# Float32 attention queries by five products of 64 columns, in place of a zero fill and fifteen bfloat16 products

## The reference

```python
x = _layernorm(x + _L0_gnn_ref(x, edge_index, ...))    # two sage_conv layers, relu between
Qh = (x @ Wq.T + bq).reshape(n, H, D)                  # H = 4 heads of D = 16
Kh, Vh = (x @ Wk.T + bk).reshape(n, H, D), (x @ Wv.T + bv).reshape(n, H, D)
Ee = (edge_attr @ We.T + be).reshape(-1, H, D)
score = (Kh[src] * Qh[dst] * (1.0 / np.sqrt(D)) * Ee).sum(-1)
score = jnp.exp(jnp.clip(score, -5.0, 5.0))
msg = Vh[src] * score[..., None]
wV = jax.ops.segment_sum(msg, dst, num_segments=n)
out = _layernorm(x + wV.reshape(n, H * D))
```

## Time and profile before

| | us |
|---|---|
| median of 3 runs | 13896.76 (13885.14 to 13908.0) |
| the profiled execution | 13876.17 |
| its span | 13874.4 |

### The profile page before, as it was taken

How to read it: one execution, slowest core, us unless ns; L and a number is a source line. 1 busy time by engine, 2 the same in 40 slices (tenths; PEclk the granted TensorE clock), 3 DMA queues, 4 the chain that set the end, 5 groups by cost and what they waited for, 6 DMA issues and landing times.

```text
span 13874.4 us, 192542 instructions
## 1 busy us (share of the span) xinstructions
PE 7655.9 (55%) x51633; PEld 6718.6 (48%) x51634; DVE 4877.0 (35%) x11774; ACT 2823.4 (20%) x4770; POOL 7767.2 (56%) x8221
## 2 busy tenths in 40 slices
PE   5556656566666555566655555444444544444554
PEld 4555545555555445455544545444444444444444
DVE  3333333333333323233333334333333333433334
ACT  1111111111111000000000003333333333333333
POOL 5555655555555555555555555555555555555554
PEclk7666666766666666666666666555555555555555
DMA  3222222222222112111111112333333333333333
GB/s 62 50 55 52 53 50 50 49 50 49 49 49 49 42 41 46 41 42 43 41 40 41 40 40 82 101 97 98 101 95 98 98 99 90 101 92 93 99 93 82
DMA packets 951617, 917.13 MB, mean 66 GB/s; under 512 B 484896, under 2 KB 740544, under 8 KB 950544
## 3 DMA queue, kind: packets, MB, share of 16 engines
q0 software_dynamic: 260000, 369.16, 12.8%
q1 hardware_dynamic: 605345, 430.43, 11.6%
q10 hardware_dynamic: 85325, 105.63, 2.2%
HBM read 789.35 MB, written 115.24 MB: 65 GB/s over the span
## 4 chain that ended last, share of the span: by engine, by line
PE 30%; issue 30%; another core or an unknown queue 23%; DVE 7%; DVEq 7%; ACT 2%; ACTq 0%; DMA 0%; POOL 0%; POOLq 0%; SPq 0%
PE ps_kv L763 4%; PE ps_kv L754 3%; PE ps_e L740 3%; PE ps_sum L723 2%; PE ps_q L723 2%; PE ps_kv L923 2%; PE ps_hot L723 2%; PE ps_t L732 1%; ACT node_q L1037 1%; PE ps_kv L772 1%; PE ps_sum L923 1%; PE ps_hot L923 1%; PE ps_kv L903 1%; PE ps_q L923 1%
## 5 line engine op out<-in xcount | busy, mean ns | idle before, releaser
L627 POOL DMA_INDIRECT kv<-kv_rows,src_ids x3125 | 2955.6, 946 | 2344.0 <-DVE message L1520 1412.2
L627 POOL DMA_INDIRECT kv<-in_x,src_ids x2500 | 2365.3, 946 | 1845.4 <-issue 912.1
L627 POOL DMA_INDIRECT kv<-h_rows,src_ids x2500 | 2367.1, 947 | 1801.5 <-issue 955.6
L754 PE MATMUL ps_kv<-between,hot 128*128 128x490 bf16 x2500 | 897.8, 505 | 976.2 <-ACT node_q L1037 553.9
L723 PE MATMUL ps_sum<-kv,hot 128*128 128x65 f32 x5000 | 937.9, 355 | 247.7 <-issue 210.5
L723 PEld LDWEIGHTS ps_sum<-kv,hot 128*128 128x128 f32 x5000 | 922.8, 277 | 270.9 <-issue 270.2
L1086 ACT ACTIVATE node_h<-node_h,unit 128x640 bf16<-128x640 f32 x722 | 1042.6, 1444 | 36.9 <-issue 8.1
L723 PE MATMUL ps_hot<-kv 128*128 128x65 f32 x1880 | 418.9, 400 | 1075.4 <-issue 885.8
L723 PEld LDWEIGHTS ps_hot<-kv 128*128 128x128 f32 x1880 | 391.7, 309 | 1148.8 <-issue 1146.7
L754 PEld LDWEIGHTS ps_kv<-between,hot 128*128 128x128 bf16 x2500 | 291.4, 130 | 1305.9 <-issue 995.8
L1306 DVE TENSOR_SCALAR between<-ps_t,message 128x980 bf16<-128x980 f16 x1250 | 898.7, 719 | 0.0
(11 more groups left out here) (253 smaller groups left out, 12432.2 us busy)
## 6 DMA issues: line engine op xcount, KB each, us to landing
node_h<-in_dst SPq DMA_DIRECT2D x625, 320.0 KB
node_q<-in_edge_attr SPq DMA_DIRECT2D x125, 480.0 KB
edge_space<-ee_rows SPq DMA_DIRECT2D x125, 480.0 KB
kv<-kv_rows,src_ids POOLq DMA_INDIRECT x3125
kv<-in_x,src_ids POOLq DMA_INDIRECT x2500
node_q<-in_edge_attr SPq DMA_DIRECT2D x125, 320.0 KB
kv<-h_rows,src_ids POOLq DMA_INDIRECT x2500
edge_space<-ee_rows SPq DMA_DIRECT2D x125, 320.0 KB
```

The lines of the kernel that those rows point to most:

```text
L627: nc.gpsimd.indirect_dma_start(out=into_slot, out_offset=None, in_=table_rows, in_offset=bass.IndirectOffsetOnAxis(ap=ids, axis=0),).then_ ...
L754: mm = nc.tensor.matmul(bank, place_hot[:, k, :], pair_hot[:, k, half * HALF * W:(half + 1) * HALF * W], start=(k == 0), stop=(k == K - 1))
```

## The change

Queries are kept in float32, and TensorE multiplies them with float32 one-hots.

- `queries32` (float32, 64 columns a block) lies over `node_q`; VectorE writes it, without `raw_queries`, without waits for room. `split_queries` and its semaphores go; ScalarE and VectorE wait for `d_kvq.read` in their place.
- `hotT` and `hotT_x` become float32, `q_block` 64 float32 columns. The Square reads `edge_ids` with the stride of five elements and writes `hotT` directly, the Relu works in place there; `apart` and the wait for the previous Relu go.
- `query_rows` issues five products a group in place of fifteen, and as many for an extra block in place of fifteen.
- The zero fill (L910) goes. `sum_messages` starts the bank (start=True) and doesn't end it when queries follow (`last`), so that the first query product of a column writes and later ones add. The three starting products (L951) stay open likewise.

```diff
@@ -118,6 +118,7 @@
 
         tiles_a, tiles_b = ((end - first) * EE_A for first, end in PARTS)
         sums_space = node_q[:].rearrange("p b f -> p (b f)").bitcast(F32)
+        queries32 = sums_space[:, 0:NB * D].rearrange("p (b f) -> p b f", b=NB)
         at = EE_A * 2 * PAIRS * D
         attr = sums_space[:, 0:at].rearrange("p (i f) -> p i f", i=EE_A)
         edge_space = sb("edge_space", [P, max(tiles_b, SLOTS) * K * D], F32)
@@ -181,20 +182,18 @@
         at = SLOTS * K * P
         hot32_x = after_h[:, at:at + K * P].rearrange("p (k n) -> p k n", k=K)
         at += K * P
-        hotT_x = after_h[:, at:at + K * P // 2].bitcast(BF16).rearrange("p (k n) -> p k n", k=K)
-        at += K * P // 2
-        q_block_x = after_h[:, at:at + ROW // 2].bitcast(BF16)
-
-        at += ROW // 2
+        hotT_x = after_h[:, at:at + K * P].rearrange("p (k n) -> p k n", k=K)
+        at += K * P
+        q_block_x = after_h[:, at:at + D]
+        at += D
 
         edge_ids = after_h[:, at:at + SLOTS * K * P].bitcast(I32).rearrange("p (u e) -> p u e", u=SLOTS)
         at += SLOTS * K * P
-        hotT = after_h[:, at:at + SLOTS * K * P // 2].bitcast(BF16).rearrange("p (u k e) -> p u k e", u=SLOTS, k=K)
-        at += SLOTS * K * P // 2
-        q_block = after_h[:, at:at + SLOTS * ROW // 2].bitcast(BF16).rearrange("p (u f) -> p u f", u=SLOTS)
-        at += SLOTS * ROW // 2
-        apart, apart_x = after_h[:, at:at + K * P], after_h[:, at + K * P:at + 2 * K * P]
-        assert at + 2 * K * P <= NB * 2 * D
+        hotT = after_h[:, at:at + SLOTS * K * P].rearrange("p (u k e) -> p u k e", u=SLOTS, k=K)
+        at += SLOTS * K * P
+        q_block = after_h[:, at:at + SLOTS * D].rearrange("p (u f) -> p u f", u=SLOTS)
+        at += SLOTS * D
+        assert at <= NB * 2 * D
         squares = after_h[:, NB * D:].rearrange("p (b f) -> p b f", b=NB)
 
 
@@ -676,28 +670,11 @@
                 z = node_x[:, c * CH:(c + 1) * CH, D:2 * D]
                 nc.gpsimd.tensor_tensor(z, z, over_features(std[:, c * CH:(c + 1) * CH]), ALU.mult).then_inc(d.normed, 1)
 
-            def split_queries(c):
-                raw, rest = raw_queries[:, c % 2], raw_queries[:, 2]
-                into = node_q[:, c * CH:(c + 1) * CH, :]
-                pool.wait_ge(d_kvq.read, c + 1)
-                nc.gpsimd.tensor_copy(into[:, :, 0:D], raw).then_inc(split_step, 1)
-                pool.wait_ge(split_step, 3 * c + 1)
-                nc.gpsimd.tensor_tensor(rest, raw, into[:, :, 0:D], ALU.subtract).then_inc(split_step, 1)
-                pool.wait_ge(split_step, 3 * c + 2)
-                nc.gpsimd.tensor_copy(into[:, :, D:2 * D], rest).then_inc(split_step, 1)
-                pool.wait_ge(split_step, 3 * c + 3)
-                nc.gpsimd.tensor_tensor(into[:, :, 2 * D:], rest, into[:, :, D:2 * D], ALU.subtract).then_inc(split_done, 1)
-
-                pool.wait_ge(split_done, c + 1)
-
             gather(sum_x, sum_x.summed, 0, x, sum_rows, D)
             pool.wait_ge(d_one.stored, 16 * CHUNKS)
             gather(sum_h, sum_h.summed, 1, h_rows, sum_rows, D)
             for c in range(CHUNKS):
                 scale(c, d_two)
-                if c > 0:
-                    split_queries(c - 1)
-            split_queries(CHUNKS - 1)
             pool.wait_ge(d_kvq.stored, 16 * CHUNKS)
             gather(att, att.message, 2, kv_rows, kv, 2 * D)
             for c in range(CHUNKS):
@@ -899,15 +876,12 @@
             def query_rows(to, turned, block_rows):
 
                 for k in range(K):
-                    for s in range(SPLIT):
-                        mm = nc.tensor.matmul(to[:, k * D:(k + 1) * D], turned[:, k, :], block_rows[:, s * D:(s + 1) * D],
-                                              start=False, stop=False)
+                    mm = nc.tensor.matmul(to[:, k * D:(k + 1) * D], turned[:, k, :], block_rows, start=False, stop=False)
                 return mm
 
             def queries(p, x, g, u, word):
 
                 pe.wait_ge(p.hot_c, g + 1)
-                nc.tensor.matmul(ps_query[u][:, 0:K * D], ones16[:], zeros16[:], start=True, stop=False)
                 query_rows(ps_query[u], hotT[:, u], q_block[:, u])
                 before, first, more = word
                 with pe.If(more):
@@ -918,9 +892,9 @@
 
                 nc.tensor.matmul(ps_query[u][:, 0:1], ones16[:], zeros16[:, 0:1], start=False, stop=True).then_inc(p.query, 1)
 
-            def sum_messages(to, one_hots, messages):
+            def sum_messages(to, one_hots, messages, last=True):
                 for k in range(K):
-                    mm = nc.tensor.matmul(to, one_hots[:, k, :], messages[:, k, :], start=(k == 0), stop=(k == K - 1))
+                    mm = nc.tensor.matmul(to, one_hots[:, k, :], messages[:, k, :], start=(k == 0), stop=(last and k == K - 1))
                 return mm
 
             def extra_sums(x, word, u):
@@ -939,16 +913,17 @@
                         g = t * SLOTS + u
                         of = (u - 1) % SLOTS
                         pe.wait_ge(p.message, g + SLOTS)
-                        sum_messages(ps_node[(u + QUERIES) % SLOTS], hot32[:, of], message[:, of])
+                        queries_follow = not (last and u + QUERIES >= SLOTS)
+                        sum_messages(ps_node[(u + QUERIES) % SLOTS], hot32[:, of], message[:, of], last=not queries_follow)
                         extra_sums(x, words[u], of)
-                        if not (last and u + QUERIES >= SLOTS):
+                        if queries_follow:
 
                             pe.wait_ge(p.scored, g + 1)
                             queries(p, x, g + QUERIES, (u + QUERIES) % SLOTS, words[u + QUERIES + 1])
 
                 words = group_words(ENG.PE, 0, 0, QUERIES)
                 for g in range(QUERIES):
-                    nc.tensor.matmul(ps_node[g], ones16[:], zeros16[:, 0:D], start=True, stop=True)
+                    nc.tensor.matmul(ps_node[g], ones16[:], zeros16[:, 0:D], start=True, stop=False)
                     queries(p, x, g, g, words[g])
                 with pe.Fori(0, TURNS - 1) as t:
                     turn(t, False)
@@ -1076,17 +1051,17 @@
 
             nc.scalar.activation(unused[:], zero[:], ACT.Sqrt)
             layer_two(d_two, d_kvq)
-            act.wait_ge(split_done, CHUNKS)
+            act.wait_ge(d_kvq.read, CHUNKS)
             p, x = att, extra
 
-            def block_edges(apart, into, ids, b, done, count, ready):
-
-                nc.scalar.activation(apart, ids, ACT.Square, bias=opposite[:, bass.ds(b, 1)]).then_inc(done, 1)
+            def block_edges(into, ids, b, done, count, ready):
+
+                nc.scalar.activation(into, ids.rearrange("n (e k) -> n k e", k=K), ACT.Square, bias=opposite[:, bass.ds(b, 1)]).then_inc(done, 1)
                 act.wait_ge(done, count)
-                nc.scalar.activation(into, apart.rearrange("n (e k) -> n k e", k=K), ACT.Relu, bias=unit[:], scale=-1.0).then_inc(ready, 1)
+                nc.scalar.activation(into, into, ACT.Relu, bias=unit[:], scale=-1.0).then_inc(ready, 1)
 
             def block_queries(into, b):
-                nc.scalar.copy(into.rearrange("p (a f) -> p a f", a=1), node_q[:, bass.ds(b, 1), :])
+                nc.scalar.copy(into.rearrange("p (a f) -> p a f", a=1), queries32[:, bass.ds(b, 1), :])
 
             def prepare(g, turn, u, word):
 
@@ -1094,9 +1069,7 @@
                 act.wait_ge(p.ids[u], turn * 16 + 16)
                 hold(act)
                 block_queries(q_block[:, u], block_at(first))
-                if not (isinstance(g, int) and g == 0):
-                    act.wait_ge(p.hot_c, g)
-                block_edges(apart, hotT[:, u], edge_ids[:, u], block_at(first), p.apart, g + 1, p.hot_c)
+                block_edges(hotT[:, u], edge_ids[:, u], block_at(first), p.apart, g + 1, p.hot_c)
                 with act.If(more):
                     with act.Fori(0, more) as j:
                         n = before + j
@@ -1104,7 +1077,7 @@
                         act.wait_ge(x.query, n + 1)
                         hold(act)
                         block_queries(q_block_x, block_at(first + j + 1))
-                        block_edges(apart_x, hotT_x, edge_ids[:, u], block_at(first + j + 1), x.apart, n + 1, x.hot_c)
+                        block_edges(hotT_x, edge_ids[:, u], block_at(first + j + 1), x.apart, n + 1, x.hot_c)
 
             def weights(t, last):
                 words = group_words(ENG.Activation, t, -(QUERIES + 1), SLOTS)
@@ -1468,13 +1441,10 @@
             v.memset(stage[D:D + 1, :, :], 1.0).then_inc(d_kvq.meant, 1)
 
             def queries(c):
-                if c >= 2:
-
-                    dve.wait_ge(split_done, c - 1)
                 for i, (first, count, part) in enumerate(kvq_parts):
 
                     dve.wait_ge(d_kvq.ready, len(kvq_parts) * c + i + 1)
-                    read = v.tensor_scalar_mul(raw_queries[:, c % 2, first:first + count, :],
```

(1 more changed line is left out.)

## The result

The changed kernel takes 13800.9 us (median of 11 runs, 13778.7 to 13832.6) against 13891.4 (11 runs) of the kernel before on the same chip: ratio 0.9938, interval 0.9925 to 0.9951. It is 0.6% faster; 14130 us, 1.8% slower, was forecast. The time lies inside the range given (13740 to 14510), the sign is wrong. Repeated beside a kernel before of 13730.7 us the ratio was 0.9943 (0.9927 to 0.9960).

A forecast was written before the change was run, and what follows sets the result against it. Attention was held bound by slow issue to TensorE during GpSimd's long gather runs, no engine being full. 13876.2 + 258 (attention) - 1 (layer two) = 14133, said as 14130 us; range 13740 to 14510.

The forecast's parts named there:

- TensorE's work: In attention, TensorE's work a group was to rise from 4.16 to 5.28 us.
- the 0.18 off for slow stretches: In attention, 0.18 us a group taken off TensorE's work, as lone float32 passes hide less waiting.
- the extra blocks' 131 us: In attention, 97 groups' extra query blocks each pay TensorE 2.17 instead of 0.82 us: +131 us.
- D: Rival: dense float32 passes in attention raise TensorE's clock; -120 us, 13755 us; chance 0.07.
- ScalarE: In attention, query copy, Square and Relu take 2.0 to 3.2 us, below TensorE's 4.40: 0 on the path.
- Layer two: GpSimd's four splitting operations a chunk go, 14 times: gain 0 to 4 us, 1 taken.
- s - e = 4.73: In attention: TensorE's fed time from a gather run's start, less its delay until refed after the run: 4.73 us.
- A: Rival: gather runs in attention keep their length; idle stays 4.36 us a group; 14595 us; chance 0.25 with or without C.
- B: Rival: gather runs in attention fall apart into single groups; at n = 1.4, -211 us, 13665 us; chance 0.18.
- n = 1.8: In attention, groups that GpSimd gathers in one run before it stops: 2.50 before, 1.8 forecast.
- C: Rival: slow issue in attention hangs on instructions, not time; -100 us, with A 14495 us; chance within A's 0.25.
- E: Rival: TensorE isn't attention's pace, its added work fills idle time; no change, 13876 us; chance 0.06.

The follow-up runs named there:

- short15: The kernel before with fifteen more bfloat16 products of 64 columns a group that add zeros: 14411.6 us, ratio 1.0374.
- wide3: The kernel before with three more bfloat16 products of 320 columns a group that add zeros: 14035.5 us, ratio 1.0111.

## Why the prediction was wrong

- **TensorE's work: right.** 5.28 us a group forecast, 5.25 measured; ten query passes in 2.13 us (11022.00 to 11024.13), no zero fill. Its parts weren't told apart, the 0.18 off for slow stretches among them. One of them has a slip: the extra blocks' 131 us belong to the window's 564 groups, so they are 0.23 us a group, not 0.21.
- **The clock: right.** 0.50 in the window, so D is out. In the changed kernel with a fifth of the gathers TensorE was busy for 2397.82 of 2400 us at 0.50. By the rule cited for D that stretch should have had the full clock (the Trainium skill, "TensorE: Matmul & The Clock Gate", "Why this matters for your kernels"); for float32 passes of 64 columns the trace says no: they stayed at 1.2 GHz. In layer two, among other products, such passes do run at 0.91; what makes the difference was not tested.
- **ScalarE: right.** 1.45 + 0.83 + 0.24 = 2.52 us, within 2.0 to 3.2, and not on the path.
- **Layer two: in its bounds.** From the last gather of the sums to the first of attention it is 125.3 us against 127.7, a gain of 2.3 where 1 was taken and 0 to 4 given.
- **s - e = 4.73, held fixed: the step that failed.** The prediction took the end of the fed time as GpSimd's own, a time after the start of a run, and used it as a constant both in the forecast and in A and B. It is 7.5 us in the changed kernel. What goes by the age of the run is when VectorE's issue turns slow (7.2 and 7.8 us); TensorE goes on for some 50 rows, 6.0 us of the old mix and 11.0 us with float32 queries. The two cases that the prediction read, 5.9 and 9.5 us, were taken as scatter of a time; counted in the same trace they are 46 and 50 rows, the longer one because it holds the message sums of an extra block and 1.56 us of idle time. At n = 2.44 the old constant gives 5.25 + 6.25 - 4.73 / 2.44 = 9.56 us a group, the measured one is 8.42: the mis-sized term is worth 1.1 us a group, some 710 us. The last sentence of the prediction's list of what would make it wrong named this and gave it no price.
- **n = 1.8: wrong, and it hid part of the first error.** 229 stops were measured, 310 forecast, worth 0.7 us a group the other way. The likely cause is the same, that TensorE is still fed when a second and a third message are due; no run takes it apart.
- **A** was right that runs keep their length and wrong in the price (14595), again by the constant. **C** was right that instructions matter (short15 against wide3), and looked for them inside the slow stretch; most of their worth lies ahead of it, in the rows that TensorE still executes. **B** didn't happen: no run of fewer than 1.88 groups on average was seen without a pause, and its break-even moved with s - e: 5.25 + 6.25 - 7.5 / n = 8.49 at n = 2.49, so runs of 2.44 groups lie just on the faster side. **E** is refuted by short15 and by the runs with a fifth of the gathers, though its time was 76 us off.

What stays open: why the engines issue slowly in a long run of gathers, and why not on one chip. In what was compared nothing differs between the chips but the gaps: gathers are 1.25 us apart and VectorE's L1237 takes 0.88 us on both. No run took it apart further.

## What to carry to other kernels

Where an engine is starved by slow issue and not by data, count the time that its instructions carry, not the busy time alone: fewer and longer instructions bridge a slow stretch, even when they are more work. Before holding a measured constant fixed through a change, ask which of the changed things it could be made of; here one term made of instructions held was mis-sized by 710 us, where the whole change gives 90. And look for what triggers the slow stretch: a pause of 1.5 us on the engine that isn't late gave the kernel before 3.0%, five times what the change gives, on the chips that have the slow issue.

## What was not expected of the hardware

- In all sets of runs but one, some seven us of gathers by indirect DMA without a pause slow the issue of the other engines: VectorE's to 0.70 us a register instruction, TensorE's to a row in 2.79 us (11034.62 to 11037.41). On one chip they don't. The kernel before takes 13731 to 13898 us on the others and 10445 on that one, so a quarter of its time is at stake, 1900 to 2050 us of it ahead of attention.
- TensorE executes far more instructions than VectorE before it runs out: 46 to 52 rows, each a weight load and a product, from the start of a run, where VectorE has executed about 40 instructions, register ones included, at its first slow one (medians, in the kernels of the table of rows). The Trainium skill, page "Runtime: NRT & Kernel Launch", section "Instruction fetch mechanics", gives TensorE's instruction memory four times the size of the others'; the direction agrees, and no run here shows that memory.
- ScalarE's read with a step of five elements costs 1.45 us for 640 columns against 0.83 without, whether it stands in the Square or in the Relu (L1059, L1061; the earlier trace rows), for int32 and for float32.
